# State-space layer: decays in a ring of four banks, read products one unit late, r + e added by a DMA, gates late, residual rows added by TensorE

## What is computed

```
xz = x @ W_in.T;  xp, z = split(xz)
xc = silu(conv1d(xp) + conv_b)                 # 4 taps, 384 channels
dt, Bt, Ct = split(xc @ W_xproj.T)             # 12, 16, 16
dt = softplus(dt @ W_dt.T + b_dt)
A  = -exp(A_log)
h  = exp(dt * A) * h + (dt * xc) * Bt          # over time, 16 states n per channel
y  = sum_n h * Ct + xc * D
y  = y * silu(z);  out = y @ W_out.T
result = h_in + 0.5 * (out_fwd + out_bwd)
```

## Time and profile before

| what | value |
|---|---|
| median of 3 runs | 4825.98 us (4822.94 to 4830.41) |
| the profiled execution, its own time | 4824.94 us |
| its span | 4823.1 us |
| TensorE busy | 4354.2 us (90%) |
| GpSimd busy | 3184.9 us (66%) |
| VectorE busy | 3395.9 us (70%) |
| ScalarE busy | 2378.0 us (49%) |
| state-space layer | about 1130 to 3930 us of the span |

### The profile page before, as it was taken

How to read it: one execution, slowest core, us unless ns; L and a number is a source line. 1 busy time by engine, 2 the same in 40 slices (tenths; PEclk the granted TensorE clock), 3 DMA queues, 4 the chain that set the end, 5 groups by cost and what they waited for, 6 DMA issues and landing times. The chain is left out here.

```text
span 4823.1 us, 62759 instructions
## 1 busy us (share of the span) xinstructions
PE 4354.2 (90%) x17088; PEld 2262.3 (47%) x17088; DVE 3395.9 (70%) x5016; ACT 2378.0 (49%) x4078; POOL 3184.9 (66%) x1637
## 2 busy tenths in 40 slices
PE   7999986996999999999999999999999975999994
PEld 4666644663334343343434334343433333666673
DVE  5677763111899999999999999999999985111114
ACT  3555542122665665656666565666656534122221
POOL 3222212441998999999999999999999951444441
PEclk9999997997999999999999999999999987999997
DMA  1000012342232233333223233222323221333456
GB/s 34 20 23 20 16 61 64 110 131 77 84 110 99 98 109 103 102 100 105 99 102 109 100 106 100 105 98 102 109 100 105 97 80 35 106 116 116 124 168 217
DMA packets 262442, 453.11 MB, mean 94 GB/s; under 512 B 38892, under 2 KB 175932, under 8 KB 262300
## 3 DMA queue, kind: packets, MB, share of 16 engines
q1 hardware_dynamic: 235776, 403.02, 25.3%
q0 software_dynamic: 23424, 48.00, 3.2%
q10 hardware_dynamic: 3100, 0.64, 0.1%
HBM read 409.75 MB, written 41.81 MB: 94 GB/s over the span
## 5 line engine op out<-in xcount | busy, mean ns | idle before, releaser
L1765 POOL TENSOR_TENSOR m_xh<-m_u,m_Bb 128x1536 f32<-128x1536 f32 x512 | 1753.0, 3457 | 223.4 <-DVE m_u L1639 223.0
L1694 PE MATMUL bank<-m_xh,ident 128*128 128x512 f32 x3072 | 1443.5, 605 | 26.3 <-POOL m_xh L1754 26.3
L1721 ACT ACTIVATE bank<-m_dt,m_Ac 128x508 f32<-128x508 f32 x1536 | 1019.2, 683 | 416.5 <-DVE bank L1736 281.1
L1736 DVE TENSOR_TENSOR_SCAN bank<-bank,m_xh 128x512 f32<-128x512 f32 x864 | 1060.1, 1227 | 36.3 <-ACT bank L1721 7.8
L1694 PEld LDWEIGHTS bank<-m_xh,ident 128*128 128x128 f32 x3072 | 568.5, 192 | 807.9 <-issue 730.7
L1736 DVE TENSOR_TENSOR_SCAN m_xh<-bank,m_xh 128x512 f32<-128x512 f32 x672 | 774.1, 1205 | 31.8 <-ACT bank L1721 27.7
L1754 POOL TENSOR_TENSOR m_xh<-m_xh,m_Cb 128x1536 f32<-128x1536 f32 x224 | 774.4, 3457 | 11.0 <-DVE m_xh L1736 10.6
L1745 DVE TENSOR_TENSOR m_xh<-bank,m_Cb 128x512 f32<-128x512 f32 x864 | 597.8, 692 | 69.3 <-DMA m_Cb<-BC_rows 23.9
L1204 ACT ACTIVATE f1t_h<-bank,f1t_b 128x512 f32<-128x512 f32 (+1 forms) x276 | 147.9, 587 | 509.7 <-PE bank L1234 509.7
L1553 PE MATMUL bank<-m_xp,m_dg 128*128 128x512 f32 x768 | 349.9, 598 | 3.2 <-ACT m_xc L1561 2.6
L1134 POOL DMA_INDIRECT rows_y<-f1t_y,f1t_home x142 | 139.9, 985 | 317.6 <-DVE f1t_y L1175 288.4
(11 more groups left out here) (366 smaller groups left out, 6138.1 us busy)
## 6 DMA issues: line engine op xcount, KB each, us to landing
m_Bb<-BC_rows SPq DMA_DIRECT2D x256, 512.0 KB, 4.7
m_Cb<-BC_rows SPq DMA_DIRECT2D x256, 512.0 KB, 3.9
f1t_w<-f_w SPq DMA_DIRECT2D x46, 576.0 KB
f1t_w1a<-f_w SPq DMA_DIRECT2D x46, 384.0 KB
f0t_w<-f_w SPq DMA_DIRECT2D x22, 576.0 KB
f1c_yg<-rows_y SPq DMA_DIRECT2D x16, 768.0 KB, 8.3
f1t_w1b<-f_w SPq DMA_DIRECT2D x92, 96.0 KB
f0t_w1a<-f_w SPq DMA_DIRECT2D x22, 384.0 KB
```

Source lines behind the costliest of these rows:

```text
L1694: mm = pe.matmul(bank[:, c, :], K.ident[:, :], xh[n % NX][:, c, :], start=False, stop=(d == 1 and n == NS - 1))
L1721: act.activation(o[:, :, lo:hi], seqs(dt[d][:, c, :])[:, :, lo:hi], ACT.Exp, scale=Ac[:, c, n:n + 1]).then_inc(s_dA, 1)
L1736: dve.tensor_tensor_scan(o, bank[:, 3 + p % 3, way], xh[n % NX][:, c, way], 0.0, ALU.mult, ALU.add).then_inc(s_h, 1)
L1765: pool.tensor_tensor(xh[n % NX][:, :, :], u[d][:, :, :], Bb[q % RB][:, n % QN, :].unsqueeze(1).to_broadcast([P, DC, TOK]), ALU.mult).then_ ...
```

## The change

- The table of decay banks becomes a ring of four, RING[d][p], banks 3 to 6. A scan that VectorE reads itself now writes in place over its decay bank, and the read (`dve_read`, new L1787) stands one unit later: scan p + 1, then read p. `released` tells ScalarE what to wait for before it writes a bank again. The zero at a sequence's edge must be written again wherever the scan overwrote it. Bank 6 carries the expert rows between units 7 and 15.
- BY_POOL is one list for each direction: eight states for d = 0, six for d = 1 (14 a group, as before).
- r = r + e is made by an accumulating DMA that GpSimd issues (`pool_add`, new L1652, once a slot, 128 x 1536 floats, in SBUF). `pe_sp` has three products a chunk instead of four: w1, lw, then r, and the first of r waits for the DMA.
- W_out is scaled by 0.5 once. `pe_out` adds the residual rows H by an identity product (new L1746), and ScalarE copies the bank back to H (`act_out`), where VectorE did a fused multiply-add.
- The gate products stand last, behind `dt`; Silu of the gates moves to the next slot (`act_gz`); the waits of `pe_proj`, `pe_dt`, `pe_gate` and `pe_out` on bank 7 follow the new order. Nearly all numbers of POS change.

```diff
         POS = {
-            "y": (6, 9, 11), "pe_D0": (7, 11, 12), "pe_D1": (11, 23, 30), "pe_out": (17, 18), "out": (19, 22),
...
-            "act_xc": (19, 22), "act_e": (27, 32), "act_w1": (30, 34), "act_ln": (31, 35), "pe_sp0": (31, 36, 41),
-            "act_sp0": (36, 41, 42), "u0": (35, 39, 42), "pe_sp1": (38, 40, 42), "act_sp1": (39, 42, 43), "u1": (38, 40, 42),
+            "y": (7, 8, 9), "pe_D0": (11, 13, 17), "pe_D1": (7, 20, 29), "pe_out": (11, 16), "out": (13, 19),
...
+            "act_pj": (15, 10), "act_xc": (13, 8), "act_e": (24, 24), "act_w1": (25, 28), "act_ln": (27, 29),
+            "pe_sp0": (28, 36, 42), "act_sp0": (29, 38, 42), "u0": (29, 38, 40), "pe_sp1": (32, 35, 40), "act_sp1": (33, 38, 41),
+            "u1": (33, 38, 41),
         }
-        BY_POOL = (0, 3, 4, 7, 10, 12, 15)
+        BY_POOL = (0, 3, 4, 5, 10, 11, 12, 14), (2, 4, 6, 10, 11, 14)
+        RING = ((3, 4, 5, 6) * 2 + (3, 4, 5, 3, 4, 5, 3) + (6, 4, 5, 3) * 8 + (6,),
+                (4, 5, 3, 6, 4, 3, 5, 6) + (3, 4, 5, 6) * 10)
+        ROWS_BANK, ROWS_FROM, ROWS_TO = 6, 7, 15
...
+        def released(act, g, d, p):
+            n, c = divmod(p, DC)
+            if n in BY_POOL[d]:
+                act.wait_ge(s_h, (g * 2 + d) * UNITS + p + 1)
+            else:
+                act.wait_ge(s_prv, dve_reads(g, d, n) + c + 1)
...
+            def pool_add(pool):
+                pool.wait_ge(s_e, s + 1)
+                stand_alone(pool, K.go)
+                pool.dma_start(r[:, :, :].rearrange("p c t -> p (c t)"), e[d][:, :, :].rearrange("p c t -> p (c t)"),
+                               accum_op=ALU.add).then_inc(s_er, 16)
...
-                for k, t in enumerate((r, e[d], w1[d], lw)):
-                    mm = pe.matmul(bank[:, front(c), :], K.ident[:, :], t[:, c, :], start=(k == 0), stop=(k == 3))
+                for k, t in enumerate((w1[d], lw, r)):
+                    if c == 0 and t is r:
+                        pe.wait_ge(s_er, (s + 1) * 16)
+                        stand_alone(pe, K.go)
+                    mm = pe.matmul(bank[:, front(c), :], K.ident[:, :], t[:, c, :], start=(k == 0), stop=(k == 2))
...
+            put("pool", POS["act_e"][d] + 1, pool_add)
...
-                                   wo[:, c, :], start=(c == 0), stop=(c == DC - 1))
+                                   wo[:, c, :], start=(c == 0), stop=False)
+                mm = pe.matmul(bank[:, NB, (j % 2) * C:(j % 2 + 1) * C], K.ident[:, :],
+                               H[:, bass.ds(g * G + j, 1), :].rearrange("p a c -> p (a c)"), start=False, stop=True)
...
-                o = bank[:, 6, way]
-                if later(g, d) or p > 0:
-                    dve.wait_ge(s_prv, (g * 2 + d) * READS + reads(n) + c)
-            dve.tensor_tensor_scan(o, bank[:, 3 + p % 3, way], xh[n % NX][:, c, way], 0.0, ALU.mult, ALU.add).then_inc(s_h, 1)
+                o = bank[:, RING[d][p], way]
+            dve.tensor_tensor_scan(o, bank[:, RING[d][p], way], xh[n % NX][:, c, way], 0.0, ALU.mult, ALU.add).then_inc(s_h, 1)
...
-        def dve_out(dve, g, i):
-            dve.wait_ge(s_ops, g * 2 + i + 1)
-            hs = H[:, bass.ds(g * G + 2 * i, 2), :]
-            dve.scalar_tensor_tensor(hs, bank[:, NB, 0:2 * C].rearrange("p (j c) -> p j c", j=2), 0.5, hs,
-                                     ALU.mult, ALU.add).then_inc(s_out, 1)
+        def act_out(act, g, i):
+            act.wait_ge(s_ops, g * 2 + i + 1)
+            act.copy(H[:, bass.ds(g * G + 2 * i, 2), :], bank[:, NB, 0:2 * C].rearrange("p (j c) -> p j c", j=2)).then_inc(s_out, 1)
...
                 def main(dve, g, d, p, end):
                     dve_scan(dve, g, d, p)
-                    if p // DC not in BY_POOL:
-                        dve_read(dve, g, d, p)
+                    if later(g, d) or p > 0:
+                        dve_read(dve, *((g, d, p - 1) if p > 0 else (g, 0, UNITS - 1) if d == 1 else (g - 1, 1, UNITS - 1)))
```

More of the change, by code:

```diff
@@ L1375, in mamba_phase @@
+            "act_rows": (11, 13), "rows": (12, 14), "stats": 14, "rstd": 17, "norm": 40,
[3 rows of a table added]
+            "act_pj": (15, 10), "act_xc": (13, 8), "act_e": (24, 24), "act_w1": (25, 28), "act_ln": (27, 29),
+            "pe_sp0": (28, 36, 42), "act_sp0": (29, 38, 42), "u0": (29, 38, 40), "pe_sp1": (32, 35, 40), "act_sp1": (33, 38, 41),
+            "u1": (33, 38, 41),
         }
         NB = 7
-        BY_POOL = (0, 3, 4, 7, 10, 12, 15)
-        ROWS_IN = 3
-        pool_reads = lambda n: sum(k < n for k in BY_POOL)
@@ L1380, in mamba_phase, with before_in_bank @@
-        reads = lambda n: DC * (n - pool_reads(n))
-        READS, POOL_READS = reads(NS), pool_reads(NS)
+        BY_POOL = (0, 3, 4, 5, 10, 11, 12, 14), (2, 4, 6, 10, 11, 14)
+        RING = ((3, 4, 5, 6) * 2 + (3, 4, 5, 3, 4, 5, 3) + (6, 4, 5, 3) * 8 + (6,),
+                (4, 5, 3, 6, 4, 3, 5, 6) + (3, 4, 5, 6) * 10)
+        ROWS_BANK, ROWS_FROM, ROWS_TO = 6, 7, 15
+        def before_in_bank(d, p):
+            b, back = RING[d][p], 0
+            while True:
+                p -= 1
+                if p < 0:
+                    p, d, back = UNITS - 1, 1 - d, back + 1
+                if RING[d][p] == b:
+                    return back, d, p
@@ L1382, in mamba_phase @@
+        of_pool = lambda d, n: sum(k < n for k in BY_POOL[d])
+        of_dve = lambda d, n: DC * (n - of_pool(d, n))
+        pool_reads = lambda g, d, n: g * (of_pool(0, NS) + of_pool(1, NS)) + d * of_pool(0, NS) + of_pool(d, n)
+        dve_reads = lambda g, d, n: g * (of_dve(0, NS) + of_dve(1, NS)) + d * of_dve(0, NS) + of_dve(d, n)
         of_q = lambda q: range(q * QN, (q + 1) * QN)
-        FIRST_POOL = [min((n % QN for n in of_q(q) if n in BY_POOL), default=None) for q in range(NQ)]
-        FIRST_DVE = [min((n % QN for n in of_q(q) if n not in BY_POOL), default=None) for q in range(NQ)]
+        first_pool = lambda d, q: min((n % QN for n in of_q(q) if n in BY_POOL[d]), default=None)
@@ L1385, in mamba_phase @@
+        first_dve = lambda d, q: min((n % QN for n in of_q(q) if n not in BY_POOL[d]), default=None)
         PW = P + 2 * (TAPS - 1)
@@ L1462, in act_rows @@
                         stand_alone(act, K.go)
-                        act.wait_ge(s_prv, g * 2 * READS + reads(ROWS_IN))
+                        released(act, g, 0, ROWS_FROM)
                 else:
                     act.wait_ge(s_added, gl * 2 + 1)
-                act.copy(bank[:, 6, 0:2 * C], z[:, 2 * i:2 * i + 2, :].rearrange("p j c -> p (j c)")).then_inc(s_copied, 1)
+                act.copy(bank[:, ROWS_BANK, 0:2 * C], z[:, 2 * i:2 * i + 2, :].rearrange("p j c -> p (j c)")).then_inc(s_copied, 1)
             def dve_rows(dve, i):
@@ L1565, in act_xc @@
                 act.activation(xc[d][:, :, :], xc[d][:, :, :], ACT.Silu).then_inc(s_xc, 1)
-                if d == 1:
-                    act.wait_ge(s_zc, g * DC + DC)
-                    act.activation(gz[:, :, :], gz[:, :, :], ACT.Silu).then_inc(s_gz, 1)
+                if d == 0 and not first:
+                    act_gz(act, g - 1)
                 act.preload_act_table_set("natural_log_exp_and_others")
@@ L1590, in pe_dt @@
                     pe.wait_ge(s_pj, s + 1)
+                    if d == 1 and deep:
+                        stand_alone(pe, K.go)
+                        pe.wait_ge(s_out, g * 2)
                 elif not first:
@@ L1689, in pe_sum @@
         def pe_sum(pe, g, d, n, c):
[L1690 to L1691 removed]
+            if n not in BY_POOL[d]:
+                pe.wait_ge(s_prv, dve_reads(g, d, n) + c + 1)
             elif c == 0:
[L1693 removed]
+                pe.wait_ge(s_prp, pool_reads(g, d, n + 1))
             mm = pe.matmul(bank[:, c, :], K.ident[:, :], xh[n % NX][:, c, :], start=False, stop=(d == 1 and n == NS - 1))
@@ L1843, in program @@
             before(eng)
+            end = {"pe": [], "act": [(POS["act_xc"][0], act_gz, (NG - 1,))], "dve": [], "pool": []}
             def group(g, last):
                 slot(eng, name, g, 0, chain(g, 1, norm=not last)[name], main, last)
-                slot(eng, name, g, 1, [] if last else chain(g + 1, 0)[name], main, last)
+                slot(eng, name, g, 1, end[name] if last else chain(g + 1, 0)[name], main, last)
             group(0, False)
@@ L1882, in main, with after @@
                     act_decay(act, g, d, p)
-                program(act, "act", main, lambda act: None, lambda act: None)
+                    if d == 0 and later(g) and p in POS["out"]:
+                        act_out(act, g - 1, POS["out"].index(p))
+                def after(act):
+                    for i in two:
+                        act_out(act, NG - 1, i)
+                program(act, "act", main, lambda act: None, after)
             @block.gpsimd
@@ L1909, in main @@
                             dve_y(dve, g - 1, POS["y"].index(p))
-                        elif p in POS["out"]:
-                            dve_out(dve, g - 1, POS["out"].index(p))
```

(3 more changed lines are left out.)

51 lines of the change are left out of this document (30 added, 21 removed), and 6 rows, old and new, of the table POS.

## The result

4752.19 us, median of 4 runs (4748.08 to 4757.64), against 4824.46 for the kernel before on the same chip: ratio 0.9846, 95% interval 0.9834 to 0.9858, 72 us faster. Forecast: 4766, range 4700 to 4830.

A forecast was written before the change was run, and what follows sets the result against it. VectorE was taken as the bound, 168.8 of 169.1 us a group. After: GpSimd's 160.8 plus DMA wait 3.8 plus half a microsecond gives 165.1, 4.0 less; 15 groups save 60 us, so 4766, range 4700 to 4830.

The forecast's parts named there:

- VectorE was the bound and is not any more: VectorE, per group: load 163.5 plus waits 5.3 fill 168.8 of 169.1 us; after the change load 149.1, 154.4 with waits.
- The pair: VectorE, a scan and a read: 1.74 us instead of 1.99 once each stands behind an instruction it does not need.
- GpSimd is next, with its wait for u gone: GpSimd, per group: load 158.2 plus two DMA issues of 1.3 gives floor 160.8 us; the 10.1 wait for u goes.
- The DMA's landing is the new wait, before the read of state 10: GpSimd in slot d = 1: waits 3.8 us once a group for the accumulating DMA, through u and scans 30 to 32.
- D: Time from issue to landing of the accumulating DMA: taken as 7.7 us, between 3.9 and 12.
- the formula D - 3.9: GpSimd's wait in slot d = 1: it arrives 10.2 us after the issue and may go on after D + 6.3.
- rival 3: VectorE gains nothing from the new order, since each instruction drains as before: 18 us less, 4808 us; chance 0.07.
- TensorE at 154, 7 below GpSimd: TensorE, per group: 158 less 5.2 for six products plus 1.5 for four residual products; 7 us room for its waits.
- No wait in the other slot up to D = 12: Slot d = 0: eight GpSimd products (27 us) before the last u, softplus needs D + 14, so no wait.
- ScalarE: nothing on the path: ScalarE's added copies cost nothing; at its long Silu block VectorE may wait a microsecond or two, with 6 to spare.
- The ends cancel: Layer ends: the last read falls from 3.4 to 0.7 us, the first chain waits some 3 us longer for its DMA.
- The rival that ended slower: The DMA lands late, D over 12: a group takes 160.8 + D - 3.9, 4867 us at D = 15; chance 0.14.

The follow-up runs named there:

- e3: The changed kernel without the accumulating DMA, softplus summed by four products a chunk again: 4751.2 us, ratio 0.9840.
- e4: The changed kernel with VectorE's read back directly behind its own scan, ring of four banks kept: 4805.4 us, ratio 0.9954.
- e5: The changed kernel with the accumulating DMA of the other chain (slot d = 0) issued two products later, behind state 12: 4834.1 us, ratio 1.0014.
- e2: The changed kernel with the accumulating DMA of slot d = 1 issued one GpSimd product later, behind state 11: 4810.6 us, ratio 0.9966.
- e7: The changed kernel without residual products; VectorE adds bank and H in place of ScalarE's copy, at the same units 13 and 19: 4847.6 us, ratio 1.0043.
- e12: As e7, with the residual rows added by VectorE at units 11 and 14 instead of 13 and 19: 4785.3 us, ratio 0.9916.
- e1: The changed kernel with the accumulating DMA of slot d = 1 issued one GpSimd product earlier, behind state 9: 4695.6 us, ratio 0.9728.

## Why the prediction was right

- *VectorE was the bound and is not any more*: right, but its proof was not one. Load plus waits gave 168.8 of 169.1 for VectorE, and it gives the period on every engine: TensorE 162.2 + 6.9, GpSimd 158.2 + 10.1. What pointed at VectorE was that it waited least and that GpSimd waited for it. The runs decide: e3 reaches the whole 5.0 us a group with TensorE as busy as before the change, and e4 loses 3.6 of them without the late read. So the late read carries most of the result, as far as e4 can tell with its clock at 0.50 more often; ring, new places and relief were not parted, and no run has the new places alone. The pair was forecast at 1.74, it is 1.72. (The forecast took the short gap behind all 54 reads; before the change only some 38 of them had the long one of 0.72.)
- *GpSimd is next, with its wait for u gone*: right, 10.1 a group became 0.4 to 0.6. The issue was taken at 1.3 and moves the next product by 0.6 to 0.7 only.
- *The DMA's landing is the new wait, before the read of state 10*: right in place and form. D was forecast at 7.7 from two SP transfers (their slope of 1.4 us for 448 KB gives 7.9):

```profile
m_r<-m_dt POOLq DMA_DIRECT2D x32, 768.0 KB, 6.9
```

  With 6.9 the formula D - 3.9 gives 3.0, and the waits before reads are 3.0 a group. At the place itself it is 2.64 in the group shown: GpSimd arrives 11.0 behind the issue, not 10.2, since the issue takes time itself, and may go on after D + 6.8, not D + 6.3; the rest is small waits elsewhere. The group is 1.0 below the forecast of 165.1, which over 15 groups is the 14 us by which the forecast was high: D gives 0.8 of it and the two cheaper issues about as much, and the wait that stayed at the turn of the slots takes back 0.6. In part the closeness is luck. The Trainium skill (DMA: Bandwidth & Descriptors, "Anatomy of one DMA — SWDGE (gpsimd) path") gives an estimate of 3.8 us; this accumulate lands 3 us later than that, so the estimate from rows was the better one.
- *The drain that cannot be avoided* (the Trainium skill, VectorE: DVE Perf Modes, "The DRAIN you can't avoid"): rival 3 falls. Two neighbours that do not depend on each other start 1.13 and 0.59 apart, dependent ones 1.27 and 0.72. An instruction behind one that it does not need starts sooner by 0.13 to 0.14. The section itself says that an instruction which is not held starts earlier, and the forecast left that out.
- *TensorE at 154, 7 below GpSimd*: mis-sized by 4. Its load was counted from pitches of long runs, 158 before and 154 after; over 14 groups it is busy 162.2 and 157.8 us a group (2209.24 / 14), 2 below GpSimd's 159.9. So it has 6 us for all its stops and 3.4 go at the DMA. "It makes them up from its 7 us" held only just, and in e3 (162 busy, 164.5 a group) it is the fullest engine.
- *No wait in the other slot up to D = 12*: wrong. The step followed u and GpSimd and left out TensorE, which comes to the r product 9.4 us behind the issue and stands there from then on; e5 costs 5.9 us a group where 0 to 3 was expected.
- *ScalarE: nothing on the path*: right for the total, but VectorE waits 8.7 us a group for decays (60.2 and 19.0 over 9.14), not one or two. It is hidden in VectorE's new slack.
- *The ends cancel*: right. The span is 75.3 us shorter, 15 groups of 5.0.
- The rival that ended slower priced a late landing one for one. e2 shows 4.2 for 3.4, with the clock at 0.50 behind its stop of 5.7 us.

## What to carry to other kernels

Count each engine's load per period in pitches and name its waits, but do not take the sum for a proof: load plus waits is the period on every engine. Ask which engine waits least and whom the others wait for, then give work to it or take work from another (e4, e3): only that shows the bound. A handoff's price lies in where its two ends stand in the order of their engines: ask when the input was ready, not only when the result is needed. Here e had been ready five us before GpSimd came to issue the DMA, and one product earlier raised the gain from 72 to 131 us. And an instruction moved to another engine at the same place of a hand-made order moves in time by what one engine runs ahead of the other.

## What was not expected of the hardware

- TensorE's granted clock falls to 0.50 behind single stops amid a stretch at 1.00 and is back 3 to 7 us later. Behind stops of about 5.7 us (e2) and 4.1 to 4.5 (e5) it fell in every group. Behind stops of about 3.2 to 3.6 it fell in every group of e7 and e12, but in only three of the 14 of the changed kernel. The length of the stop does not tell there: it fell behind one of 3.25 and not behind one of 3.56. In those three GpSimd's wait at the read was 3.3 to 3.5 us, in the others about 2.6. In e1 and e3, without such stops, it did not fall.
- The three GpSimd products behind the DMA's issue take 10.43 and 10.51 us where three take 10.24 in the kernel before and 10.26 elsewhere in this one, so the DMA costs GpSimd 0.2 to 0.3 us beyond the issue.
- A scan in place over its own PSUM operand costs what one into another bank did (1.22 us beside 1.23), so the ring needs no bank of its own for results.
